# A graph layer's node stage: the conv times sine step by tensor_scalar, the small chains moved to GpSimd, x in one layout, the last groups normalized on three engines

## The reference, cut to what matters

```python
def _L0_gnn_ref(node_input, node_attr, edge_attr, edge_scalars, ...):     # N = E = 50000
    ...
    mid = jax.ops.segment_sum(edge_feat, edge_dst, num_segments=N) / np.sqrt(16.0)
    mid_s, mid_v = (mid[:, :96], mid[:, 96:].reshape(N, 96, 3))
    c_s, c_v = _fctp(mid_s, mid_v, node_attr, lin2_w0, lin2_w1)
    conv = jnp.concatenate([c_s, c_v.reshape(N, -1)], -1)                 # (N, 160)
    scfeat = jnp.concatenate([sc_s, sc_v.reshape(N, -1)], -1)             # (N, 160), x times weights
    angle = 0.1 * (mid_s @ lin3_w) * (1.0 / np.sqrt(96.0)) * node_attr
    return jnp.cos(angle) * scfeat + jnp.sin(angle) * conv
x = _layernorm(x + _L0_gnn_ref(...), axis=-1)       # (x - mean) / sqrt(var + 1e-5)
```

## Time and profile before

| | us |
|---|---|
| median of the runs | 1848.68 |
| the profiled execution | 1855.24 |
| its span, first to last instruction | 1853.4 |
| GpSimd busy in the span | 1358.1 |
| TensorE (matmul) busy | 1303.1 |
| VectorE busy | 1048.9 |
| ScalarE busy | 751.1 |

### The profile page before, as it was taken

How to read it: one execution, slowest core, us unless ns; L and a number is a source line. 1 busy time by engine, 2 the same in 40 slices (tenths; PEclk the granted TensorE clock), 3 DMA queues, 4 the chain that set the end, 5 groups by cost and what they waited for, 6 DMA issues and landing times.

```text
span 1853.4 us, 34160 instructions
## 1 busy us (share of the span) xinstructions
PE 1303.1 (70%) x8134; PEld 1136.0 (61%) x8134; DVE 1048.9 (57%) x4746; ACT 751.1 (41%) x1715; POOL 1358.1 (73%) x1004
## 2 busy tenths in 40 slices
PE   7767666666676876777677777768776277777773
PEld 5656666565565766666566666657665156666563
DVE  4654544544445555555555555565554198777785
ACT  3433333332333333333333333333332035666668
POOL 3347777767777777777777777777775489888885
PEclk9988888887778899989998889898998588888887
DMA  7974444444444444444444444444445557778763
GB/s 287 357 258 62 63 63 60 63 61 59 62 61 65 69 66 69 70 70 69 68 69 69 70 69 68 68 69 69 69 69 156 159 207 270 265 266 315 280 221 150
DMA packets 166687, 230.68 MB, mean 124 GB/s; under 512 B 50225, under 2 KB 135281, under 8 KB 163057
## 3 DMA queue, kind: packets, MB, share of 16 engines
q1 hardware_dynamic: 91088, 164.49, 27.1%
q0 software_dynamic: 75264, 64.68, 26.0%
q10 hardware_dynamic: 288, 1.00, 0.1%
HBM read 132.67 MB, written 97.40 MB: 124 GB/s over the span
## 4 chain that ended last, share of the span: by engine, by line
DMA 51%; issue 19%; POOL 12%; DVE 7%; PE 5%; ACT 3%; POOLq 1%; SPq 1%; DVEq 0%; ACTq 0%
DMA acc<-shared,row_sb 30%; DMA shared<-x_odd,src_sb 9%; DMA shared<-acc 7%; POOL shared L344 6%; DMA acc<-zeros 5%; POOL acc L360 5%; ACT shared L618 2%; PE XTZ L499 2%; DVE shared L830 2%; DVE ang L761 1%; DVE stats L840 1%; POOL rstd L402 1%; POOL shared L409 1%; POOL shared L415 1%; DVE turns L767 0%
## 5 line engine op out<-in xcount | busy, mean ns | idle before, releaser
L360 POOL DMA_INDIRECT acc<-shared,row_sb x392 | 644.8, 1645 | 234.0 <-issue 139.7
L499 PE MATMUL XTZ<-constants_sb,shared 128*128 128x128 f32 x588 | 127.1, 333 | 387.6 <-DMA shared<-x_odd,src_sb 387.5
L722 DVE TENSOR_TENSOR shared<-shared 128x192 f32<-128x192 f32 x196 | 70.5, 360 | 543.3 <-ACT shared L578 540.5
L499 PEld LDWEIGHTS XTZ<-constants_sb,shared 128*128 128x128 f32 x588 | 71.6, 161 | 423.5 <-DMA shared<-x_odd,src_sb 420.2
L344 POOL DMA_INDIRECT shared<-xa,src_sb x196 | 202.2, 1032 | 123.6 <-DMA src_sb<-src 56.3
L588 ACT COPY shared<-XTZ 128x384 f32<-128x384 f32 x196 | 93.9, 479 | 458.6 <-PE XTZ L499 458.6
L443 PE MATMUL OC<-shared 128*128 128x161 f32 x1176 | 242.7, 352 | 2.4 <-DVE shared L686 1.2
L344 POOL DMA_INDIRECT shared<-x_odd,src_sb x196 | 196.2, 1001 | 59.7 <-issue 46.0
L453 PE MATMUL OC<-constants_sb,shared 128*128 128x193 f32 x784 | 229.5, 379 | 0.0
L443 PEld LDWEIGHTS OC<-shared 128*128 128x128 f32 x1176 | 207.9, 230 | 10.0 <-issue 6.7
L618 ACT ACTIVATE shared<-shared,shift,rstd 128x160 f32<-128x160 f32 x392 | 170.4, 510 | 51.8 <-DVE shift L819 51.8
(11 more groups left out here) (78 smaller groups left out, 2744.4 us busy)
## 6 DMA issues: line engine op xcount, KB each, us to landing
acc<-zeros SPq DMA_DIRECT2D x50, 644.0 KB, 5.8
out<-shared SPq DMA_DIRECT2D x98, 320.0 KB, 5.1
xn_sb<-xa SPq DMA_DIRECT2D x12, 2254.0 KB, 9.1
shared<-acc SPq DMA_DIRECT2D x12, 2254.0 KB, 16.1
dstrow_sb<-dst_rows SPq DMA_DIRECT2D x196, 128.0 KB, 3.4
acc<-shared,row_sb POOLq DMA_INDIRECT x392
xl_sb<-x_last SPq DMA_DIRECT2D x12, 448.0 KB, 9.8
xn_sb<-xa SPq DMA_DIRECT2D x2, 1610.0 KB, 9.3
```

The lines of the kernel that those rows point to most:

```text
L360: pool.indirect_dma_start(out=acc, out_offset=bass.IndirectOffsetOnAxis(ap=row_sb[:, slot, j:j + 1], axis=0), in_=comb_sb[:, slot, j, :], ...
L499: last = nc.tensor.transpose(XT[:, b * P:(b + 1) * P], x_sb[:, a.slot(UNROLL), column:column + P], ident_sb[:, :])
```

## The change

Batches are now 2, 5, twelve of 7, then 4, 2 and 1.

- **Conv times sine** is four tensor_scalar instructions a group, each on one tile of 160 columns with the sine as a scalar per partition, in place of one tensor_tensor of 640 columns with a broadcast. **Adding x** is two tensor_tensor instructions (4 x 128 and 4 x 32 columns).
- **x has one layout** for the node stage, `x_node`: for each group of four tiles the first 128 columns of each, then the last 32 of each, then the four attributes. One load takes the place of two, and the copy `x_last` is gone.
- **The angle chain** (now seven instructions, since the two scalar_tensor_tensor become tensor_scalar and tensor_tensor) and `scale_trig` (now two instructions) move from VectorE to GpSimd. The angle's links stand one by one between the big instructions of the first and second group of the batch.
- **pow is gone.** VectorE makes a first guess of 1/sqrt with integer arithmetic on the bits (one more instruction after `vareps`), and GpSimd refines it with three Newton rounds of four instructions each, one by one between the big instructions from the fourth group on.
- VectorE's `variance` is now spread one by one over the second group. `rstd` and `shift` have four buffers in place of two, and y's ring has 20 groups.
- **The last 14 groups** are normalized by three engines: of a group's four tiles ScalarE takes the first, GpSimd two, VectorE the last.

```diff
-    small = [2, BATCH - 2]
-    sizes = small + [BATCH] * ((groups - 2 * BATCH) // BATCH) + small[::-1]
+    first, last = [2, BATCH - 2], [BATCH - 3, 2, 1]
+    sizes = first + [BATCH] * ((groups - 2 * BATCH) // BATCH) + last
...
-                sp.dma_start(xn_sb[:, b % LOADED, 0:count * G, :], batch_rows(xa, b)).then_inc(xn_in[b % LOADED], 16)
-                sp.dma_start(xl_sb[:, b % LOADED, 0:count * P], batch_rows(x_last, b).rearrange("p j c -> p (j c)")
-                             ).then_inc(xl_in[b % LOADED], 16)
+                rows = x_node[g * G * P:(g + count) * G * P, :].rearrange("(p i j) c -> p i (j c)", p=P, j=G)
+                sp.dma_start(xn_sb[:, b % LOADED, 0:count, :], rows).then_inc(xn_in[b % LOADED], 16)
...
                 sp.wait_ge(norm_done, s + 1)
+                if s >= NG - TAIL_GROUPS:
+                    sp.wait_ge(norm_pool, s + 1 - (NG - TAIL_GROUPS))
+                    sp.wait_ge(norm_dve, s + 1 - (NG - TAIL_GROUPS))
...
-                pool.tensor_tensor(out=rstd[:, b % 2, 0:count * G], in0=vareps[:, b % 2, 0:count * G],
-                                   in1=minus_half[:, 0:count * G], op=ALU.pow).then_inc(rstd_done, 1)
+            def root_of(b):
+                n, at = BATCHES[b][1] * G, b * REFINE
+                v, t = vareps[:, b % 2, 0:n], fix[:, 0:n]
+                pool.wait_ge(eps_done, b + 1)
...
+                for r in range(3):
+                    better = (root[:, 0, 0:n], root[:, 1, 0:n], rstd[:, b % STAGED, 0:n])[r]
...
+                    pool.tensor_tensor(out=t, in0=y, in1=y, op=ALU.mult).then_inc(refined, 1)
+                    yield
+                    pool.wait_ge(refined, at + 4 * r + 1)
+                    pool.tensor_tensor(out=t, in0=t, in1=v, op=ALU.mult).then_inc(refined, 1)
+                    yield
+                    pool.wait_ge(refined, at + 4 * r + 2)
+                    pool.tensor_scalar(t, t, -0.5, 1.5, ALU.mult, ALU.add).then_inc(refined, 1)
+                    yield
+                    pool.wait_ge(refined, at + 4 * r + 3)
+                    last = pool.tensor_tensor(out=better, in0=y, in1=t, op=ALU.mult)
...
+            def conv_times_sine(b, i, j):
+                n = i * G + j
+                tile = pool.tensor_scalar(cs_sb[:, b % LOADED, n, 0:ROW], cs_sb[:, b % LOADED, n, 0:ROW],
+                                          trig_a[:, b % 2, 1, n:n + 1], None, ALU.mult)
...
+                for i in range(count):
+                    links = ahead if i < 2 else behind if i > 2 else iter(())
+                    for j in range(G):
+                        if i + 1 < count:
+                            conv_times_sine(b, i + 1, j)
+                        next(links, None)
+                    for half in range(2):
+                        add_x(b, i, half)
+                        next(links, None)
+                    if i == 3 and not scaled:
+                        scale_trig(b + 1)
+                        scaled = True
```

248 lines of the change are left out of this document (152 added, 96 removed).

## The result

| | before | after |
|---|---|---|
| median of the runs | 1848.57 | 1989.89 |
| lowest to highest | 1847.55 to 1850.75 | 1988.12 to 1992.6 |
| span of the profiled execution | 1853.4 | 1990.8 |

The change makes the kernel **7.6% slower**: ratio 1.0764, 95% interval 1.0745 to 1.0783. The forecast was 1806 with a range up to 1842.

The account below looks back on a forecast made before the run. The bound was taken to be overlapping cycles with waits, period 25.7 us, falling to 22.8. Batches saving 32.6 us and the tail 9.1, called 42, taken from 1848.7 gave 1806.7, stated as 1806; range 1784 to 1842.

Parts of the forecast that it names:

- c, the tensor_scalar: Conv times sine on GpSimd: each 160-column tensor_scalar costs 0.25 us, 28 of them 7.0 us a batch for 8.7.
- s and a: GpSimd: s, a small 28-column link, 0.14 us; a, adding x in two instructions, 1.34 us a group.
- The rival that came true: GpSimd's fixed cost over 63 instructions a batch makes the kernel slower: period 29.9 us, 1894 us; chance 0.11.
- f: Fixed cost of each GpSimd instruction in the slower rival: gain turns to loss at 0.23 or 0.14 us; priced at 0.25.
- The load cycle: Load of acc, angle links to red, sines and next load's issue: 15.2 + 3.3 + 3.1 = 21.6 us for 25.7.
- The variance cycle: VectorE's statistics, GpSimd's Newton rounds, shift, normalization, products, next y: 22.8 us, longest of three, taken as the period.
- the mis-sized term: In the variance cycle, VectorE's sixth group, 2.3 us.
- The cover: The sixth group's y and statistics on VectorE, under which the Newton rounds run; named as what is late next.
- The port: VectorE's small instructions beside GpSimd: each wait ends at a GpSimd instruction boundary, one every 0.25 to 1.1 us.
- The end: After the last x addition, with normalization split over three engines: 14.5 us for 23.6, saving 9.1.
- if the first 14 stores still queue: Warning on the end: 14 stores of 320 KB are 10.6 us of DMA, so the saving would be 7 us, not 9.1.
- the edge stage's end: Sign to check: the edge stage should be the same within 3 us.

Follow-up runs that it names:

- e4: Kernel before, with a probe of single GpSimd instruction forms (tensor_scalar with one or two operations, several widths) added after its last work: 1855.99 us, one run.
- e9: Kernel before, with pow replaced by a first guess on VectorE and twelve Newton links on GpSimd: 1839.56 us, ratio 0.9966.
- e10: Kernel before, with x in one layout (one load for two) and x added in two instructions: 1877.17 us, ratio 1.0133.
- e13: Kernel before, with Newton links for pow and the angle chain's first product moved from VectorE to GpSimd: 1863.68 us, ratio 1.0086.
- e11: Kernel before, with Newton links for pow and x in one layout: 1851.86 us, ratio 1.0022.
- e8: Kernel before, with the angle chain and scale_trig moved to GpSimd: 1858.65 us, ratio 1.0059.
- e1: Changed kernel, with conv times sine put back to one broadcast tensor_tensor: 1877.98 us, ratio 1.0127 to the kernel before.
- e7: Kernel before, with the last 14 groups normalized by two engines, two tiles each on ScalarE and VectorE: 1849.37 us, ratio 0.9997.

## Why the prediction was wrong, point by point

**c, the tensor_scalar: the step that failed.** It was set at 0.25 us, "nearer to the memset's side, since one input is read and not two". It measured 0.66. A memset reads nothing and computes nothing; the bound from above was then taken as 1.95 ns a column plus a fixed cost of 0.03 to 0.10, from memsets again. Both parts were wrong: the fixed cost of this form is 0.25 us, and one operation is 2.5 ns a column (e4). 28 x 0.41 is 11.5 us a batch, which turns the sum for GpSimd from 19.3 to 30.8 by itself. With that GpSimd is busy without a pause and its own work is the period, where the prediction had it wait for the variance.

**s and a.** A link is 0.22 for 0.14, the addition of x 1.54 for 1.34. Together 21 x 0.08 + 7 x 0.20 = 3.1: 33.9 in all, 11 us over the 22.8 that the longest of the three cycles was given.

**The rival that came true** is the first, with a chance of 0.11: GpSimd bounds, through fixed cost. Its f of 0.25 is what the tensor_scalar turned out to have. Its price, 1894, was too low: its period of 29.9 took the middle of 0.83 and 1.95 ns a column, where the tensor_scalar has 2.5, and it kept the end's gain of 9 us, which did not come. The two rows for a fixed cost were `pow`'s 0.40 us at no columns and the memsets' 0.03. What was measured, 0.25 for the tensor_scalar and 0.19 to 0.20 for a link of four columns, lies between them, and the prediction took the memsets' side.

**The load cycle** was right as a mechanism: in e9, e10 and e13 its three parts laid end to end are the distance of two load issues. Taking the copy of x away brought 0.6 us (e10, medians) to 0.9 (e11 beside e9), for 1.1 predicted. The angle's links on GpSimd took 6.0 us from the first link to the end of `red` in e8, where a big instruction of 1.3 us stands behind each pair of links, and 6.3 in the changed kernel (1510.39 to 1516.70), for 3.3; in e1, without the slow product, 4.8 (1712.04 to 1716.82). In the changed kernel the tensor_scalars between the links are a part of that; in e8 there are none.

**The variance cycle.** e1 shows it, since there GpSimd no longer bounds; its period is 26.3 for the forecast 22.8 (eleven from 1538.46 to 1827.77; GpSimd is busy 90 of 100 us). The chain in order of time, one round of 25.4:

```profile
1710.39 0.53 DVE shift L904
...
1718.93 0.03 DVE shared L917
...
1723.07 0.24 POOL fix L470
...
1730.63 0.20 POOL rstd L479
...
1735.83 0.54 DVE shift L904
```

From the shift to the next batch's y 8.5 us, y and variance 4.1, Newton 7.8, and from `rstd` to the shift **5.0**. The first two are 12.7 for 5.5 + 6.0; Newton was given 9.0. The last is the mis-sized term: 2.3 was VectorE's own work in the sixth group, but on GpSimd a product with sine (1.25) and the x additions of that group (1.55) stand behind the last Newton link, and VectorE waits for them. The cover was itself late.

**The port.** VectorE's `mdiff` and its neighbours were to wait a boundary at most. In the changed kernel `m2eps` takes 1954 ns on the mean of twelve, for 158 in before, and e10 shows a wait over seven GpSimd instructions. The Trainium skill, "SBUF — State Buffer", section "Who interferes with whom", says that one engine gets the shared ports for its whole instruction and the other blocks. The traces agree on the block. In e9 they agree on its length too, since each product ends at GpSimd's next boundary; in e10 they don't, for in eight of twelve batches it waited through the stream.

**The end** was to take 14.5 us for 23.6; it took 28.1. GpSimd's and SyncE's timelines of the changed kernel:

```profile
1966.02 0.20 POOL L470 TENSOR_TENSOR fix<-guess 128x8 f32<-128x8 f32 x1 [3.35 <-DVE guess L893]
...
1969.57 6.43 POOL L511 TENSOR_SCALAR shared<-shared,rstd,shift 128x160 f32<-128x160 f32 x14 [0.22 <-POOL rstd L479]
1975.96 0.19 POOL L470 TENSOR_TENSOR fix<-guess 128x4 f32<-128x4 f32 x1
...
1979.47 6.42 POOL L511 TENSOR_SCALAR shared<-shared,rstd,shift 128x160 f32<-128x160 f32 x14 [0.22 <-POOL rstd L479]
```

```profile
1972.99 13.29 SPq L311 DMA_DIRECT2D out<-shared  x14
```

The serial Newton chain was right (3.3 us). But there are two of them and both halves of GpSimd's tiles behind the last addition, where the sum counted one of each, and a tile takes 0.46 us for 0.25: 3.4 + 3.3 + 0.2 + 6.4 + 3.3 + 0.2 + 6.4 + 4.9 = 28.1. The warning "if the first 14 stores still queue" was priced at 2.1 us of the 9.1. In e7, whose engines are quick, bunched stores take back the 1.8 us that the arithmetic won; but there the stores are bunched because VectorE begins late, so what they would take of an earlier start stays open.

**What held**: the edge stage's end moved by only 1.5 us.

## What to carry to other kernels

An instruction form of GpSimd that the trace doesn't show is priced by running it, not from a memset: here the one-operation tensor_scalar was the dearest elementwise form tried, and adding a second operation that does nothing saved 103 us. Splitting a GpSimd instruction costs 0.2 to 0.3 us a piece (the x addition in two takes 1.55 us for 1.27), and moving links off a waiting VectorE to the engine that works beside it moves the wait onto that engine's whole queue (e8, e13). Replacing one long custom operation (`pow`, 4.8 us) by twelve small ones paid 0.2 to 0.5% in e9, as far as the trace shows by what it did to VectorE's waits more than by GpSimd's shorter work, which was not the bound. Before an end is spread over engines, look at when each of them can start and whether the stores would have room.
